# A two-layer graph network: half-length rows and three built columns in the second layer's gather loop

## The chip, the cores and the metric

The kernel runs on one core of a Trainium2 chip. The metric is the device time in microseconds of one execution. Engines are named as in the profile: PE (TensorE), ACT (ScalarE), DVE (VectorE), POOL (GpSimd), SP (SyncE, which here only issues DMAs).

## What is computed

Two graph layers over 12500 nodes of 32 features and 412500 edges sorted by destination. Before each, `h = relu(layernorm(x))`; each layer's output is added to `x`. The first is attention by a softmax over each node's incoming edges. The second, on which the change bears:

```python
x = h[src]; y = h[dst]; c = w_comp[etype]                  # 86 relations, 16 bases
xb = einsum('ei,bio->ebo', x, weight)
msg = einsum('eb,ebo->eo', c, xb)                          # = x @ W[etype]
x_hat = x @ A1_w.T + A1_b
y_hat = y @ A2_w.T + A2_b + rel_emb[etype]
a = tanh(relu(sum(x_hat * y_hat, -1) / sqrt(32)))
nei = segment_sum(a[:, None] * msg, dst)
curr = h[src[last_e]] @ self_loop_weight                   # last_e: last incoming edge of the node
h_new = relu(where(in_deg > 0, nei + curr, 0))
```

## The kernel before

**Layout.** The edges are cut into 128 runs of T = 3224, one per partition. Layer 0 takes them in 52 groups of 62 columns, layer 1 in 134 groups (`GROUPS1`) of 24 columns (`K1`) and a tail of 8 (`KT`). A column is one edge on each partition. Most columns come by an indirect DMA issued by POOL (`gather`, L683), which reads one row per partition from a table in DRAM. In layer 0 a row has 33 words. Some of layer 0's columns are not gathered but built: PE multiplies one-hot masks with the table that is held in SBUF in bf16 parts (L967), DVE picks the right one of 13 candidates.

**The table of layer 1.** Between the layers (about 3590 to 4003 us) the kernel computes, for each of the 98 nodes of a partition, `h1` and its product with all relations' matrices (PE L1017 and L1018), evicts it (ACT L858 to L864, DVE L1405) to a tile `tb` and stores it (SP L600). A table row serves 16 relations (`R8`; six rows a node): 16 words of bias products, 32 of `x_hat`, 32 of the self-loop product, 16 x 32 of messages, W1 = 592 words. A node's stored part has 3232 words. The `y_hat` of each node is stored too, and scattered to where its edges start.

**One group of layer 1.** POOL gathers `KG` = 23 columns into `g1`, which has two buffers: gathers for group g+2 wait until DVE has used group g (`s_g1_free`). The 24th column is built one group ahead. Who does what:
- ACT, in `edges1(g)`: `choose(g+1)` makes the one-hot masks (eight squares L895, one L896, two relus L898 and L899); the tanh (L913); a copy of the self part (L915); `relation` (L881); `fill(g+1)`: copies the picked row's transpose to `xT` (L903), waits for the products, copies the coefficients (L906) and the node part (L907); then, after DVE's scan, `y_starts(g+1)` (L884 to L888) and the copy to `r1` (L923).
- PE, in `base(g)`: two code transposes (L1039, L1040), wait for the masks, 24 matmuls over the table (L1049) into `found1`, transpose of the picked row (L1053), product with the bases (L1055), node product (L1056), coefficients (L1057).
- DVE, in `messages(g)`: fills the `y` values by a scan (L1458), masks of the relation, logits (L1468 to L1470), four `copy_predicated` (L1475) which halve the 16 messages to one by the bits of the relation number, with `pick_row(g+1)` (L1439 to L1444) after the first; weighting (L1482), the sum by a scan (L1485), `build_row(g+1)` (L1449 to L1453), and it waits for `r1` before the next group.
- SP loads `y` values, relations and indices and stores `r1` (L628 to L634).

Each engine runs its own list in order; semaphores tie them. At the end a fix of the run borders, 98 gathers of each node's last edge (sums and self part), three DVE operations per seventh of the nodes (L1517 to L1519), and the output.

Of the kernel before, what the change touches and what calls it, by code (L numbers as in the profile page):

```python
# [15 lines left out]
bf16 = mybir.dt.bfloat16  # L16
# [23 lines left out]
KG = K1 - 1  # L40
# [4 lines left out]
R8 = 16  # L45
# [25 lines left out]
assert 2 * (GROUPS - NB + 1) == J and PB == R8 and GROUPS1 % 2 == 0 and 0 < KT < K1  # L71
assert J == LOWS * (HIGHS - 1) + TALL and COLS0 % BATCH == 0 and 2 * BATCH <= PC - AHEAD0 + 1 and HIGHS <= R8
# [15 lines left out]
def build(nc, x, src, dst, etype, attn_w, weight, w_comp, self_w, a1_w, a1_b, a2_w, a2_b, rel_emb, out):  # L88
# [14 lines left out]
    yhat_d = dram("y_hat", (NP, D))  # L103
    z1_d = dram("y_hat_at_starts", (EP, D))
    r1_d = dram("layer1_scans", (EP, 2 * D))

    with ExitStack() as ctx:
# [10 lines left out]
        yhat = agg[:, :, :].rearrange("p j c -> p (j c)")[:, 0:J * D].rearrange("p (j c) -> p j c", c=D)  # L118
        shared = sb("weights_and_zeros", [P, WC + 3 * WC // 2 + K * D // 2])
# [3 lines left out]
        zeros = shared[:, WC + 3 * WC // 2:WC + 3 * WC // 2 + K * D // 2]  # L123
# [6 lines left out]
        a1b = sb("a1_and_bias", [D, D + 1])  # L130
        wattn = sb("attention_weights", [P, 2 * D])
# [19 lines left out]
        ylast = sb("last_y_hat", [P, D])  # L151
# [53 lines left out]
        junk = sdst_e[:, 0:T]  # L205
        blocks = view(0, [SB, EB])
# [38 lines left out]
        hT = take([TB, P], bf16)  # L245
        centered = zeros[:, 0:JQ * D].rearrange("p (j c) -> p j c", c=D)
# [4 lines left out]
        z1, r1, r1t, contx, r1t_tail, contx_tail = (  # L251
            shared[:, at:at + n].rearrange("p (a b) -> p a b", b=b) for at, n, b in (
                (0, K1 * D, D), (K1 * D, 2 * K1 * D, 2 * D), (3 * K1 * D, D * (K1 + 1), K1 + 1),
                (4 * K1 * D + D, D * (K1 + 1), K1 + 1), (5 * K1 * D + 2 * D, D * (KT + 1), KT + 1),
                (5 * K1 * D + KT * D + 3 * D, D * (KT + 1), KT + 1)))
        lg = take([K1])
        av = take([K1])
        spare = h[:, :, :].rearrange("p j c -> p (j c)")
        pr = spare[:, 0:K1 * (D + R8)].rearrange("p (k c) -> p k c", c=D + R8)
        ct1 = spare[:, K1 * (D + R8):K1 * (D + R8) + 2 * P]  # L260
        cn1 = spare[:, K1 * (D + R8) + 2 * P:K1 * (D + R8) + 3 * P]
# [47 lines left out]
        zp = ps[:, 0:2, :].rearrange("p b c -> p (b c)")[:, 0:D * (K1 + 1)].rearrange("p (c k) -> p c k", k=K1 + 1)  # L309
# [1232 lines left out]
```

## Time and profile before

| | us |
|---|---|
| median of 3 runs | 8054.69 (8054.45 to 8059.46) |
| profiled execution | 8059.34 |
| its span, first to last instruction | 8057.5 |
| PE, DVE, ACT, POOL busy | 4557.2, 6079.7, 1762.7, 5825.8 |

A busy share is a mean over stages that differ. The stages: up to about 580 us the indices are prepared; to about 3550 us layer 0; to 4003 us the table; to about 7905 us the loop of layer 1; then the end. The views used below are the page, busy times by stage or by short windows, groups of instructions, waits, and the timeline of one group.

### The profile page before, as it was taken

The page shows a single profiled execution, that of the slowest core. Times are in us where ns is not written, and L with a number is a line of the kernel's source. Part 1 is how long each engine was busy: PE and PEld are TensorE (multiplying, and loading weights), DVE is VectorE, ACT ScalarE, POOL GpSimd, SP SyncE. Part 2 cuts the span into 40 slices and gives each one's busy share as a digit, 9 for nine tenths or more (in the row PEclk, how much of TensorE's full clock was granted, in tenths as well). Part 3 has the DMA queues.
Part 4 walks back from the last instruction along what each step waited for, and adds up shares of the span by engine and source line. Part 5 has one row for each costly group of instructions (what it writes and reads, how often), then busy time and mean ns, then how long its engine had stood idle before and what let it go on. Part 6 is the DMA issues. An engine that isn't in the chain of part 4 may idle for free.

```text
span 8057.5 us, 68499 instructions
## 1 busy us (share of the span) xinstructions
PE 4557.2 (57%) x22931; PEld 2398.0 (30%) x22964; DVE 6079.7 (75%) x7991; ACT 1762.7 (22%) x3756; POOL 5825.8 (72%) x6148
## 2 busy tenths in 40 slices
PE   0009999999999999967633333333333333333330
PEld 0005555555555555533311111111111111111110
DVE  8437667767767767765578888888888888888883
ACT  0001001101101101126522323333232323323330
POOL 6777777777777777744367777777777777777776
PEclk9999999999999999988866666566666665656655
DMA  4412222222222222239988888888888888888882
GB/s 103 122 42 51 63 51 51 63 51 51 63 51 51 63 51 51 63 106 402 392 255 285 285 285 285 285 285 285 285 284 285 284 285 285 284 285 284 286 284 85
DMA packets 499205, 1492.16 MB, mean 185 GB/s; under 512 B 163302, under 2 KB 224019, under 8 KB 478244
## 3 DMA queue, kind: packets, MB, share of 16 engines
q0 software_dynamic: 349440, 1012.48, 44.2%
q1 hardware_dynamic: 149411, 475.30, 15.5%
q8 instruction: 181, 2.97, 0.2%
q14 instruction: 173, 1.42, 0.1%
HBM read 1078.52 MB, written 407.69 MB: 184 GB/s over the span
## 4 chain that ended last, share of the span: by engine, by line
DVE 38%; PE 29%; POOL 15%; DMA 9%; issue 7%; ACT 2%; DVEq 0%; POOLq 0%; SPq 0%; ACTq 0%
PE ps L967 27%; DVE arena L1475 16%; POOL arena L683 14%; DMA arena<-layer_rows,edge_row_index 5%; DMA layer_rows<-arena 3%; DVE arena L1470 2%; DVE arena L1282 2%; DVE h_nodes L1290 2%; DVE arena L1266 2%; DVE h_nodes L1469 1%; DVE ps L1258 1%; DVE ps L1458 1%; DVE weights_and_zeros L1485 1%; POOL dst_score_at_starts L719 1%; DVE arena L1293 1%
## 5 line engine op out<-in xcount | busy, mean ns | idle before, releaser
L683 POOL DMA_INDIRECT arena<-layer_rows,edge_row_index x5642 | 5342.6, 947 | 1783.1 <-issue 1731.3
L967 PE MATMUL ps<-arena 128*128 128x396 bf16 (+1 forms) x10752 | 2737.4, 336 | 0.0
L1475 DVE COPY_PREDICATED arena<-ps,arena 128x6144 f32<-128x6144 uint32 (+3 forms) x540 | 1828.2, 3386 | 41.7
L967 PE MATMUL ps<-h_nodes,arena 128*128 128x396 bf16 (+1 forms) x5376 | 1806.6, 336 | 0.0
L1049 PE MATMUL ps<-aggregate_nodes,weights_and_zeros 128*128 128x384 bf16 (+1 forms) x1072 | 480.0, 448 | 1632.7 <-ACT aggregate_nodes L899 1632.7
L967 PEld LDWEIGHTS ps<-arena 128*128 128x128 bf16 x10752 | 1045.5, 98 | 783.6 <-issue 18.9
L1290 DVE TENSOR_TENSOR h_nodes<-ps,h_nodes 128x429 f32<-128x429 f32 x672 | 604.7, 900 | 810.7 <-PE ps L967 810.7
L1049 PEld LDWEIGHTS ps<-aggregate_nodes,weights_and_zeros 128*128 128x128 bf16 x1072 | 136.0, 127 | 1797.5 <-ACT aggregate_nodes L899 1668.0
L967 PEld LDWEIGHTS ps<-h_nodes,arena 128*128 128x128 bf16 x5376 | 524.1, 97 | 404.9 <-issue 9.8
L1282 DVE TENSOR_SCALAR arena<-ps,low_id 128x512 bf16<-128x512 f16 x1344 | 588.0, 479 | 22.4 <-PE ps L956 0.4
L818 ACT ACTIVATE ps<-arena 128x62 f32<-128x62 f32 x52 | 11.7, 226 | 2202.9 <-DVE arena L1254 2202.9
L1049 PE MATMUL ps<-h_nodes,weights_and_zeros 128*128 128x384 bf16 (+1 forms) x1072 | 475.7, 444 | 0.0
L1049 PE MATMUL ps<-weights_and_zeros 128*128 128x384 bf16 (+1 forms) x1072 | 466.2, 435 | 0.0
L1053 PE MATMUL ps<-identity,aggregate_nodes 128*32 128x128 f32 x134 | 51.0, 381 | 732.5 <-DVE aggregate_nodes L1444 732.5
L1293 DVE TENSOR_REDUCE arena<-h_nodes 128x33 f32<-128x429 f32 x672 | 403.3, 600 | 23.1
L1458 DVE TENSOR_TENSOR_SCAN ps<-weights_and_zeros,ps 128x800 f32<-128x800 f32 x135 | 245.7, 1820 | 228.8 <-ACT weights_and_zeros L923 228.8
L956 PE MATMUL ps<-identity_h,code 128*128 128x128 f16 x672 | 65.9, 221 | 475.6 <-DVE code L1274 389.6
L824 ACT ACTIVATE arena<-arena 128x2046 f32<-128x2046 f32 x52 | 202.8, 3901 | 466.8 <-DVE arena L1266 466.8
L1055 PE MATMUL ps<-aggregate_nodes 32*128 32x512 f32 x268 | 276.1, 1121 | 47.7 <-ACT aggregate_nodes L903 47.7
L895 ACT ACTIVATE weights_and_zeros<-ps,minus_low_id 128x128 bf16<-128x128 f16 x1072 | 287.6, 372 | 0.5 <-PE ps L1040 0.5
L1405 DVE COPY arena<-ps 128x512 f32<-128x512 f32 (+1 forms) x294 | 157.5, 575 | 161.6 <-SPq L608 93.9
L884 ACT ACTIVATE weights_and_zeros<-same_dst_as_before 128x768 f32<-128x768 f32 x135 | 113.4, 840 | 749.9 <-DVE weights_and_zeros L1485 749.9
(273 smaller groups left out, 5751.7 us busy)
## 6 DMA issues: line engine op xcount, KB each, us to landing
layer_rows<-arena SPq DMA_DIRECT2D x98, 1616.0 KB, 8.0
layer_scans<-weights_and_zeros SPq DMA_DIRECT2D x134, 768.0 KB, 5.4
arena<-layer_rows,edge_row_index POOLq DMA_INDIRECT x5642, 4.1
layer_scans<-arena SPq DMA_DIRECT2D x52, 1054.0 KB, 4.2
y_hat_at_starts<-weights_and_zeros SPq DMA_DIRECT2D x52, 992.0 KB
weights_and_zeros<-y_hat_at_starts SPq DMA_DIRECT2D x134, 384.0 KB, 5.7
layer_rows<-weights_and_zeros SPq DMA_DIRECT2D x49, 320.0 KB
edge_row_index<-row_of_edge SPq DMA_DIRECT2D x134, 12.0 KB, 5.5
```

Source lines behind the costliest of these rows:

```text
L683: pool.indirect_dma_start(tile, None, table, bass.IndirectOffsetOnAxis(ap=index, axis=0)) \
L824: act.activation(r0[:, :, 0:D + 1], by_edge(r0t), ACT.Copy).then_inc(s_r0, 1)
L895: act.activation(onehot1[:, a, :], codes_n, ACT.Square, bias=neglow[:, a:a + 1])
L967: ins = nc.tensor.matmul(found[col % 2][:, 0:wide], onehot[n % 2][:, a, c * P:(c + 1) * P], tparts[i][:, a, 0:wide], start=a == 0 and i == ...
L1049: ins = nc.tensor.matmul(found1[:, 0:wide * D], onehot1[:, a, :], rows, start=a == 0 and i == 0, stop=a == LOWS - 1 and i == PARTS0 - 1)
L1055: nc.tensor.matmul(based, xT[0:D, :], wbas.rearrange("i (b o) -> i o b", o=D), start=True, stop=True)
L1266: v.tensor_tensor_scan(flat(r0t[:, 0:D, :]), flat(x0x[:, 0:D, :]), flat(b0t), 0.0, ALU.mult, ALU.add) \
L1282: ins = v.tensor_scalar(onehot[n % 2][:, a, :], codes, lowid[:, a:a + 1], None, ALU.is_equal)
L1290: v.tensor_tensor(picked[col % 2].rearrange("p c a -> p a c"), found[col % 2].rearrange("p (a c) -> p a c", c=FP), spread(high0[g % 2][:, ...
L1293: done(v.tensor_reduce(g0[g % NB][:, KP + i, 0:FP], picked[col % 2], AX.X, ALU.add))
L1458: v.tensor_tensor_scan(flat(y), flat(same), flat(y), 0.0, ALU.mult, ALU.add).then_inc(s_z1_used, 1)
L1475: done(v.copy_predicated(rows[:, :, M1:M1 + half], spread(bits[i][:, 0:k], [P, k, half]), rows[:, :, M1 + half:M1 + 2 * half]))
```

## The change

A table row now serves 8 relations (11 rows a node) and holds 8 words of bias products, `h1` itself (32 words) with a constant 1, and 8 x 32 of messages: W1 = 297 words, 1188 bytes. `x_hat . y_hat` is computed as (h1, 1) . (A1b' y_hat): the node's `y` is stored multiplied by the first attention matrix, 33 words. The self-loop product is no longer in the rows: `r1` carries `h1`, and the product with `self_loop_weight` is made at the end for each node's last edge. DVE's selects become three, over 8 messages. Of the 24 columns of a group three are built (`NE` = 3, `KG` = 21): ACT's masks are three times as wide, PE does 72 matmuls and three times transpose, product and coefficients, DVE three picks and three builds. The built columns' codes go by DRAM from the first stage to this loop. The tiles `relp` move from PSUM to SBUF. The three searches have PSUM banks 2, 4 and 5.

```diff
-KG = K1 - 1
+NE = 3
+KG = K1 - NE
 NB = 4
 QUADS = GROUPS // NB
 F0 = D + 1
 W0 = D + 2
-R8 = 16
+R8 = 8
+NS = 16
 RP = -(-RELS // R8)
 SLOTS = RP * R8
 X1 = R8
-M1 = X1 + 2 * D
+Y = D + 1
+M1 = X1 + Y
 W1 = M1 + R8 * D
 STORED = (RP - 1) * W1 + M1 + (RELS - (RP - 1) * R8) * D
-CN = 3 * D + SLOTS
+S1 = Y + 1
+CN = S1 + SLOTS
...
             def choose(g):
                 act.wait_ge(s_spelled, g + 1)
                 if g > 0:
-                    act.wait_ge(s_found1, g)
+                    act.wait_ge(s_found1, NE * g)
                 for a in range(LOWS):
                     act.activation(onehot1[:, a, :], codes_n, ACT.Square, bias=neglow[:, a:a + 1])
-                act.activation(which_r, codes_r[0:RELS, :], ACT.Square, bias=neglow[0:RELS, 0:1]).then_inc(s_hot, 1)
+                act.activation(flat_e(which_r), codes_r[0:RELS, :], ACT.Square, bias=neglow[0:RELS, 0:1]).then_inc(s_hot, 1)
                 act.wait_ge(s_hot, 2 * g + 1)
                 act.activation(onehot1, onehot1, ACT.Relu, scale=-1.0, bias=unit)
-                act.activation(which_r, which_r, ACT.Relu, scale=-1.0, bias=unit[0:RELS, :]).then_inc(s_hot, 1)
+                act.activation(flat_e(which_r), flat_e(which_r), ACT.Relu, scale=-1.0, bias=unit[0:RELS, :]).then_inc(s_hot, 1)
 
             def fill(g):
-                act.wait_ge(s_turned, g + 1)
-                act.activation(xT[0:D, :], xTp, ACT.Copy).then_inc(s_xT, 1)
-                act.wait_ge(s_based, g + 1)
-                act.wait_ge(s_g1_free, g + 1)
-                act.activation(coef, coefp, ACT.Copy)
-                act.activation(g1[:, g % 2, KG, X1:M1], noded, ACT.Copy).then_inc(s_fill, 1)
+                for e in range(NE):
+                    act.wait_ge(s_turned, NE * g + e + 1)
+                    if NE * g + e > 0:
+                        act.wait_ge(s_based, NE * g + e)
+                    act.activation(xT, xTp, ACT.Copy).then_inc(s_xT, 1)
+                act.wait_ge(s_based, NE * (g + 1))
+                if g > 0:
+                    act.wait_ge(s_built, g)
+                act.activation(coef, coefp, ACT.Copy).then_inc(s_fill, 1)
...
             def base(g):
                 if g > 0:
                     pe.wait_ge(s_fill, g)
-                nc.tensor.transpose(codes_n, code_n[:, g:g + 1].to_broadcast([P, P]), identh[:, :])
-                nc.tensor.transpose(codes_r, code_r[:, g:g + 1].to_broadcast([P, P]), identh[:, :]) \
-                    .then_inc(s_spelled, 1)
+                for e in range(NE):
+                    nc.tensor.transpose(codes_n[:, e * P:(e + 1) * P], code_n[:, g, e:e + 1].to_broadcast([P, P]),
+                                        identh[:, :])
+                for e in range(NE):
+                    ins = nc.tensor.transpose(codes_r[:, e * P:(e + 1) * P],
+                                              code_r[:, g, e:e + 1].to_broadcast([P, P]), identh[:, :])
+                ins.then_inc(s_spelled, 1)
                 pe.wait_ge(s_hot, 2 * g + 2)
                 if g > 0:
                     pe.wait_ge(s_built, g)
-                for a in range(LOWS):
-                    wide = HIGHS if a < TALL else HIGHS - 1
-                    for i in range(PARTS0):
-                        rows = table1[i][:, a:a + LOWS * (wide - 1) + 1:LOWS, :]
-                        ins = nc.tensor.matmul(found1[:, 0:wide * D], onehot1[:, a, :], rows,
-                                               start=a == 0 and i == 0, stop=a == LOWS - 1 and i == PARTS0 - 1)
-                ins.then_inc(s_found1, 1)
-                pe.wait_ge(s_xrow, g + 1)
-                nc.tensor.transpose(xTp, xrow, ident[:, :]).then_inc(s_turned, 1)
-                pe.wait_ge(s_xT, g + 1)
-                nc.tensor.matmul(based, xT[0:D, :], wbas.rearrange("i (b o) -> i o b", o=D), start=True, stop=True)
-                nc.tensor.matmul(noded, xT, wn[:, :], start=True, stop=True)
-                nc.tensor.matmul(coefp, which_r, wrel, start=True, stop=True).then_inc(s_based, 1)
+                for e in range(NE):
+                    for a in range(LOWS):
+                        wide = HIGHS if a < TALL else HIGHS - 1
+                        for i in range(PARTS0):
+                            rows = table1[i][:, a:a + LOWS * (wide - 1) + 1:LOWS, :]
+                            ins = nc.tensor.matmul(found1[e][:, 0:wide * D], onehot1[:, a, e * P:(e + 1) * P], rows,
+                                                   start=a == 0 and i == 0, stop=a == LOWS - 1 and i == PARTS0 - 1)
+                    ins.then_inc(s_found1, 1)
+                for e in range(NE):
+                    pe.wait_ge(s_xrow, NE * g + e + 1)
+                    if e > 0:
+                        pe.wait_ge(s_xT, NE * g + e)
+                    nc.tensor.transpose(xTp, g1[:, g % 2, KG + e, X1:X1 + D], ident[:, :]).then_inc(s_turned, 1)
+                    pe.wait_ge(s_xT, NE * g + e + 1)
+                    nc.tensor.matmul(based[e], xT, wbas.rearrange("i (b o) -> i o b", o=D), start=True, stop=True)
+                    nc.tensor.matmul(coefp[:, e, :], which_r[:, e, :], wrel, start=True, stop=True).then_inc(s_based, 1)
...
+            def masks(g):
+                done(v.tensor_tensor(high1[:, :, 0:HIGHS], slots[:, 0:HIGHS].unsqueeze(1).to_broadcast([P, NE, HIGHS]),
+                                     spread(high_n[:, g, :], [P, NE, HIGHS]), ALU.is_equal))
+
+            def pick_row(g, e):
+                v.wait_ge(s_found1, NE * g + e + 1)
+                done(v.tensor_tensor(picked1, found1[e].rearrange("p (a c) -> p a c", c=D),
+                                     spread(high1[:, e, 0:HIGHS], [P, HIGHS, D]), ALU.mult))
+                v.tensor_reduce(g1[:, g % 2, KG + e, X1:X1 + D], picked1.rearrange("p a c -> p c a"), AX.X, ALU.add) \
+                    .then_inc(s_xrow, 1)
+                v.wait_ge(s_xrow, NE * g + e + 1)
+
+            def build_rows(g):
                 v.wait_ge(s_fill, g + 1)
-                v.tensor_tensor(by_base, based.rearrange("p (o b) -> p o b", b=BASES),
-                                coef[:, 0:BASES].unsqueeze(1).to_broadcast([P, D, BASES]), ALU.mult)
-                done(v.tensor_tensor(by_rel, g1[:, g % 2, KG, X1:X1 + D], coef[:, BASES:BASES + D], ALU.mult))
-                v.tensor_reduce(g1[:, g % 2, KG, M1:M1 + D], by_base, AX.X, ALU.add)
-                v.tensor_reduce(g1[:, g % 2, KG, 0:1], by_rel, AX.X, ALU.add).then_inc(s_built, 1)
+                done(v.tensor_tensor(by_rel, g1[:, g % 2, KG:K1, X1:M1], coef[:, :, BASES:BASES + Y], ALU.mult))
+                v.tensor_reduce(g1[:, g % 2, KG:K1, 0], by_rel, AX.X, ALU.add)
+                for e in range(NE):
+                    done(v.tensor_tensor(by_base, based[e].rearrange("p (o b) -> p o b", b=BASES),
+                                         coef[:, e, 0:BASES].unsqueeze(1).to_broadcast([P, D, BASES]), ALU.mult))
+                    ins = v.tensor_reduce(g1[:, g % 2, KG + e, M1:M1 + D], by_base, AX.X, ALU.add)
+                    if e < NE - 1:
+                        done(ins)
+                ins.then_inc(s_built, 1)
                 v.wait_ge(s_built, g + 1)
...
                 v.tensor_tensor(which[:, 0:k, :], spread(relp[b][:, 0:k], [P, k, R8]),
-                                slots[:, :].unsqueeze(1).to_broadcast([P, k, R8]), ALU.is_equal)
-                for i in range(3):
+                                slots[:, 0:R8].unsqueeze(1).to_broadcast([P, k, R8]), ALU.is_equal)
+                for i in range(2):
                     v.tensor_scalar(bits[i][:, 0:k], rel[:, b, 0:k], R8 >> (i + 1), None, ALU.bitwise_and)
-                done(v.tensor_scalar(bits[3][:, 0:k], rel[:, b, 0:k], 1, None, ALU.bitwise_and))
+                done(v.tensor_scalar(bits[2][:, 0:k], rel[:, b, 0:k], 1, None, ALU.bitwise_and))
+                if g + 1 < GROUPS1:
+                    masks(g + 1)
                 v.wait_ge(s_g1[b], landed)
                 rows, part = g1[:, b, 0:k, :], pr[:, 0:k, :]
-                v.tensor_tensor(part[:, :, D:D + R8], rows[:, :, 0:X1], which[:, 0:k, :], ALU.mult)
-                done(v.tensor_tensor(part[:, :, 0:D], rows[:, :, X1:X1 + D], by_edge(y), ALU.mult))
+                v.tensor_tensor(part[:, :, Y:LW], rows[:, :, 0:X1], which[:, 0:k, :], ALU.mult)
+                done(v.tensor_tensor(part[:, :, 0:Y], rows[:, :, X1:M1], by_edge(y), ALU.mult))
                 v.tensor_reduce(lg[:, 0:k], part, AX.X, ALU.add).then_inc(s_lg, 1)
-                v.tensor_copy(y[:, :, 0], r1t[:, :, K1])
-                for i in range(4):
+                v.tensor_copy(y[:, 0:D, 0], r1t[:, :, K1])
+                for i in range(3):
                     half = (R8 >> (i + 1)) * D
                     v.nop(nofuse=True)
                     done(v.copy_predicated(rows[:, :, M1:M1 + half], spread(bits[i][:, 0:k], [P, k, half]),
                                            rows[:, :, M1 + half:M1 + 2 * half]))
-                    if i == 0 and g + 1 < GROUPS1:
-                        pick_row(g + 1)
+                    if i < NE and g + 1 < GROUPS1:
+                        pick_row(g + 1, i)
...
+            for q in range(J // JQ):
+                pe.wait_ge(s_sums[q], sums_landed(q))
+                if q > 0:
+                    pe.wait_ge(s_xlastT, q)
+                for j in range(JQ):
+                    ins = nc.tensor.transpose(xTsp[:, j * P:(j + 1) * P], sums1[:, q * JQ + j, D:2 * D], ident[:, :])
+                ins.then_inc(s_xlast, 1)
+                pe.wait_ge(s_xlastT, q + 1)
+                if q > 1:
+                    pe.wait_ge(s_out, q - 1)
+                for j in range(JQ):
+                    ins = nc.tensor.matmul(selfp[q % 2][:, j, :], xTs[:, q % 2, j * P:(j + 1) * P], wself, start=True,
+                                           stop=True)
+                ins.then_inc(s_curr, 1)
...
-                v.wait_ge(s_agg1[q], 16 * JQ)
+                v.wait_ge(s_sums[q], sums_landed(q))
                 total = sums1[:, at, 0:D]
-                done(v.tensor_tensor(total, total, sums1[:, at, D:2 * D], ALU.add))
+                v.wait_ge(s_curr, q + 1)
+                done(v.tensor_tensor(total, total, selfp[q % 2], ALU.add))
```

Beside this: `tb` gets its column of ones once; `a2_w` and its bias are multiplied with `a1_w` in the first stage; the weights take 7 small loads in place of 10; DVE waits there for the store of the codes; the code that shifts the relation by 4 shifts by 3, over three columns of each group in place of one; SP loads the codes before the table's first store.

## Rows read from the trace of the kernel before

**Rows 1.** The page: busy time of each engine, share of the span, instructions.
```profile
PE 4557.2 (57%) x22931; PEld 2398.0 (30%) x22964; DVE 6079.7 (75%) x7991; ACT 1762.7 (22%) x3756; POOL 5825.8 (72%) x6148
```
**Rows 2.** Stages: length, busy PE PEld DVE ACT POOL, PEclk, DMA share, GB/s.
```profile
400.00:3500.00 3100.00, 2817.83 (x16702) 1600.86 (x16703) 2107.51 (x3641) 306.35 (x198) 2339.46 (x2465) 0.99 0.24 54
...
5000.00:6000.00 1000.00, 362.36 (x1146) 163.12 (x1146) 883.13 (x873) 303.11 (x732) 756.25 (x800) 0.60 0.89 285
```
**Rows 3.** Groups, gathers: 400 to 3500 us, then 4650 to 7850 us; busy, mean ns, idle before.
```profile
L683 POOL DMA_INDIRECT arena<-layer_rows,edge_row_index x2356 | 2232.9, 948 | 718.0 <-issue 718.0
...
L683 POOL DMA_INDIRECT arena<-layer_rows,edge_row_index x2560 | 2420.3, 945 | 779.9 <-issue 777.7 <-DMA edge_row_index<-row_of_edge 2.1
```
**Rows 4.** Waits, 4650 to 7850 us: waiting line, releaser, total, times, longest.
```profile
DVE h_nodes L1468 <- DMA arena<-layer_rows,edge_row_index: 107.7, 70, 2.8
```
**Rows 5.** Groups by form, 4650 to 7850 us: count, busy, mean ns, idle before.
```profile
L1475 DVE COPY_PREDICATED arena<-ps,arena 128x6144 f32<-128x6144 uint32 x111 | 784.2, 7064 | 0.0
...
L1049 PE MATMUL ps<-h_nodes,weights_and_zeros 128*128 128x384 bf16 x666 | 272.1, 409 | 0.0
...
L1449 DVE TENSOR_TENSOR aggregate_nodes<-ps,aggregate_nodes 128x512 f32<-128x512 f32 x112 | 77.4, 691 | 3.8
```
**Rows 6.** Timeline, ACT's part of a group up to PE's start: start, duration, idle before.
```profile
5031.46 0.84 ACT L884 ACTIVATE weights_and_zeros<-same_dst_as_before 128x768 f32<-128x768 f32 x1 [5.51 <-DVE weights_and_zeros L1485]
...
5034.58 2.15 ACT L895 ACTIVATE weights_and_zeros<-ps,minus_low_id 128x128 bf16<-128x128 f16 x8
5036.58 0.38 ACT L896 ACTIVATE aggregate_nodes<-ps,minus_low_id 86x128 f32<-86x128 f16 x1
...
5038.48 0.53 PE L1049 MATMUL ps<-aggregate_nodes,weights_and_zeros 128*128 128x416 bf16 x1 [12.08 <-ACT aggregate_nodes L899]
```
**Rows 7.** Timeline of one search (24 matmuls), the pick and the chain after it.
```profile
5010.69 0.53 PE L1049 MATMUL ps<-aggregate_nodes,weights_and_zeros 128*128 128x416 bf16 x1 [12.10 <-ACT aggregate_nodes L899]
...
5015.95 0.44 PE L1049 MATMUL ps<-h_nodes,weights_and_zeros 128*128 128x384 bf16 x1
5016.22 0.33 PE L1049 MATMUL ps<-weights_and_zeros 128*128 128x384 bf16 x1
...
5017.20 0.33 PE L1049 MATMUL ps<-weights_and_zeros 128*128 128x384 bf16 x1
...
5020.03 0.59 DVE L1442 TENSOR_TENSOR aggregate_nodes<-ps,aggregate_nodes 128x416 f32<-128x416 f32 x1
...
5021.56 0.40 PE L1053 MATMUL ps<-identity,aggregate_nodes 128*32 128x128 f32 x1 [4.04 <-DVE aggregate_nodes L1444]
...
5022.32 2.07 PE L1055 MATMUL ps<-aggregate_nodes 32*128 32x512 f32 x2 [0.36 <-ACT aggregate_nodes L903]
...
5024.31 0.69 PE L1056 MATMUL ps<-node_weights,aggregate_nodes 33*128 33x64 f32 x2
...
5024.93 0.66 PE L1057 MATMUL ps<-aggregate_nodes 86*128 86x48 f32 x2
...
5025.63 0.21 ACT L906 ACTIVATE aggregate_nodes<-ps 128x48 f32<-128x48 f32 x1 [3.36 <-PE ps L1057]
```
**Rows 8.** Short windows, columns as in rows 2; the last in the table's stage.
```profile
5017.00:5018.00 1.00, 0.53 (x4) 0.10 (x1) 1.00 (x1) 0.00 (x0) 0.70 (x2) 1.00 0.98 322
5020.00:5021.00 1.00, 0.00 (x0) 0.00 (x0) 0.93 (x3) 0.00 (x0) 0.80 (x1) 0.50 0.76 256
...
3700.00:3728.00 28.00, 22.21 (x114) 10.46 (x114) 15.13 (x36) 16.66 (x48) 13.93 (x14) 0.88 0.99 400
```
**Rows 9.** Single lines: count, duration ns min/median/max, first and last start, forms.
```profile
L884 ACT ACTIVATE weights_and_zeros<-same_dst_as_before x135: 415/843/845, 4044.3 to 7905.0; 128x768 f32<-128x768 f32 x134, 128x256 f32<-128x256 f32 x1
...
L1053 PE MATMUL ps<-identity,aggregate_nodes x134: 283/396/398, 4057.4 to 7869.1; 128*32 128x128 f32 x134
...
L1055 PE MATMUL ps<-aggregate_nodes x268: 1032/1070/1219, 4058.1 to 7870.9; 32*128 32x512 f32 x134
```
**Rows 10.** Timeline of the end: two transposes of the border fix.
```profile
7917.97 0.61 PE L1066 MATMUL ps<-identity,carry_in 128*32 128x128 f32 x2 [44.87 <-DVE carry_in L1500]
```

More of the change, by code:

```diff
@@ L205, in build @@
         junk = sdst_e[:, 0:T]
+        coded = sdst_e[:, 2400:2400 + 3 * GROUPS1 * NE // 2 + 1].bitcast(fp16)[:, 0:3 * GROUPS1 * NE]
+        coded_n, coded_h = (coded[:, i * GROUPS1 * NE:(i + 1) * GROUPS1 * NE] for i in range(2))
+        coded_r = coded[:, 2 * GROUPS1 * NE:3 * GROUPS1 * NE].rearrange("p (g e) -> p g e", e=NE)
         blocks = view(0, [SB, EB])
@@ L245, in build @@
         hT = take([TB, P], bf16)
+        of_built = take([3 * GROUPS1 * NE // 2 + 1]).bitcast(fp16)
+        code_n, high_n, code_r = (of_built[:, i * GROUPS1 * NE:(i + 1) * GROUPS1 * NE].rearrange(
+            "p (g e) -> p g e", e=NE) for i in range(3))
+        table1 = [take([J, D // 2], bf16)]
         centered = zeros[:, 0:JQ * D].rearrange("p (j c) -> p j c", c=D)
@@ L394, in build @@
         s_wplaced = sem("s_wplaced")
-        s_agg0 = [sem(f"s_agg0_{i}") for i in range(-(-(J - TB - 1) // (2 * TB)) + 1)]
+        s_sums = [sem(f"s_sums{i}") for i in range(-(-(J - TB - 1) // (2 * TB)) + 1)]
         s_h1 = sem("s_h1")
@@ L436, in build @@
         s_self = sem("s_self")
-        s_agg1 = [sem(f"s_agg1_{i}") for i in range(J // JQ)]
         s_out = sem("s_out")
@@ L749, in _ @@
             for j in range(AHEAD):
-                gather(agg[:, j, :], r0_d, last[:, j:j + 1], s_agg0[part_of[j]])
+                gather(agg[:, j, :], r0_d, last[:, j:j + 1], s_sums[part_of[j]])
             pool.wait_ge(s_zero1_d, ZEROED)
@@ L754, in _ @@
                 for i in range(j + AHEAD, min(j + AHEAD + 1, J)):
-                    gather(agg[:, i, :], r0_d, last[:, i:i + 1], s_agg0[part_of[i]])
+                    gather(agg[:, i, :], r0_d, last[:, i:i + 1], s_sums[part_of[i]])
                 pool.wait_ge(s_ev_act, 6 * j + 12)
@@ L783, in _ @@
             for j in range(J):
-                gather(sums1[:, j, :], r1_d, last[:, j:j + 1], s_agg1[j // JQ])
+                gather(sums1[:, j, :], r1_d, last[:, j:j + 1], s_sums[j // JQ])
         @block.scalar
@@ L946, in _ @@
                                  start=True, stop=True)
+            nc.tensor.matmul(ps[0:D + 1, 6, 3 * RELS:3 * RELS + Y], a2b[:, :], a1b[:, :], start=True, stop=True)
             nc.tensor.matmul(ps[0:D + 1, 6, 2 * RELS:3 * RELS], a1b[:, :], rel_t[:, :], start=True, stop=True) \
@@ L1059, in _ @@
             pe.wait_ge(s_we, 48)
             pe.wait_ge(s_table1, 1)
+            pe.wait_ge(s_codes_in, 16)
+            nc.tensor.matmul(relp1, rel_t[:, :], a1b[:, :], start=True, stop=True).then_inc(s_relw, 1)
+            pe.wait_ge(s_wrel1, 1)
             for g in range(GROUPS1):
@@ L1481, in messages @@
                 v.wait_ge(s_self, g + 1)
[L1482 removed]
+                v.tensor_tensor(by_edge(y[:, 0:D, :]), rows[:, :, M1:M1 + D], spread(avp[:, 0:k], [P, k, D]), ALU.mult) \
                     .then_inc(s_g1_free, 1)
                 v.wait_ge(s_g1_free, g + 3)
[L1485 removed]
+                v.tensor_tensor_scan(flat(scanned), flat(same[:, 0:D, :]), flat(y[:, 0:D, :]), 0.0, ALU.mult, ALU.add).then_inc(s_scan1, 1)
                 v.wait_ge(s_scan1, g + 1)
                 if g + 1 < GROUPS1:
[L1488 removed]
+                    build_rows(g + 1)
                 v.wait_ge(s_r1, g + 1)
[L1491 to L1492 removed]
+            v.wait_ge(s_codes_in, 16)
+            masks(0)
+            for e in range(NE):
+                pick_row(0, e)
+            build_rows(0)
             for it in range(0, PAIRS1):
```

208 lines of the change are left out of this document (114 added, 94 removed).

## The prediction, made before the change was run

> **What bounds the kernel now.** I read the page first. GpSimd (POOL) is busy 72% of the span and VectorE (DVE) 75%; neither share decides alone, since both are means over unlike stages [rows 1]. The table of stages then separates two long stages: layer 0 (400 to 3500 us) and the layer-1 loop, of which 5000 to 6000 us is a sample. In both POOL is busy 75 to 76% [rows 2]. The groups of gathers tell what that is: each gather lasts 0.945 to 0.948 us and is followed by 0.30 us of issue (779.9 / 2560 and 718.0 / 2356), in layer 0 with rows of 132 bytes and in layer 1 with rows of 2368 bytes [rows 3]. So a gather costs POOL 1.25 us whatever its size, and 800 gathers fill the 1000 us of the sample. The layer-1 loop has 23 gathers per group of 24 columns: 23 x 1.25 = 28.75 us. The first and last transpose of a picked row (L1053) lie 3811.7 us apart, 133 intervals, 28.66 us each [rows 9]: POOL sets the pace. But narrowly: DVE waited for gathers only 107.7 us in 111 groups, 1 us each [rows 4], and is busy 0.883 x 28.7 = 25.3 us of each.
>
> **What the change aims at.** Three columns are built instead of gathered: 21 gathers, 21 x 1.25 = 26.25 us. That alone would be worth 133 x 2.4 = 320 us. The halved row frees DMA, which bounds nothing here. It remains to see whether the other engines can run a group in 26.25 us.
>
> **DVE.** The 6144-element select goes (7.06 us); two more picks at 1.53 us (from L1442's start at 5020.03 to TensorE's at 5021.56) and two more builds of 2 x 0.69 us come, 5.8 us [rows 5, 7]; narrower masks and reduce save an estimated 0.6 us, waits between dependent steps cost about that. 25.3 - 7.06 + 5.8 + 0.6 = 24 to 25 us of work. DVE fits in 26.25 us.
>
> **ScalarE (ACT) and TensorE (PE) do not.** Their part of a group is a ring in the code, written in order on both: ACT's `choose` (one-hot masks), PE's search of the table, PE and ACT in turns through transpose, `xT`, base product and coefficients, ACT's `coef` copy in `fill`, then `y_starts` and the copy to `r1`, and only then the next `choose`. PE begins its search when the masks are there and ends with what `fill` waits for. Nothing of the ring overlaps the rest of it; before, it was shorter than DVE's and POOL's work and waited for them. Its terms now:
> - `choose`: before 3.90 us, 5034.58 to PE's start at 5038.48 [rows 6]. Eight squares and one relation mask go from 128 to 384 elements, two relus likewise (1024 to 3072, 128 to 384). ACT's slope is (843 - 415) / 512 = 0.836 ns per element [rows 9]. Added: 10 x 256 + 2048 = 4608 elements, 3.85 us. New: 7.75 us.
> - search: 72 matmuls for 24. A burst starts at the lower clock level (1.2 GHz) and goes over to 2.4 GHz within itself; the granted clock is 1.00 at its end and back at 0.50 three microseconds later [rows 8]. Spacing is (5015.95 - 5010.69) / 16 = 0.329 us low and (5017.20 - 5016.22) / 6 = 0.163 us high [rows 7]. The 384-wide ones average 409 ns [rows 5] between 530 at the low and 330 at the high level [rows 7], so about 0.41 of 18 are slow, with the six 416-wide ones 13.4 matmuls or 4.4 us. Between bursts PE rests 11.2 us in the new ring, so each burst starts low again. 13.4 x 0.329 + 58.6 x 0.163 = 14.0 us (bounds: rise at once 11.7, never 23.7).
> - three passes of the chain: at the low clock, transpose to product 0.76 us (5021.56 to 5022.32), product 1.99 us (to 5024.31), coefficients 0.70 us (5024.93 to ACT at 5025.63), of which about 0.6 before PE can go on; the node product between (0.62 us) is gone. 3.35 us a pass. They now follow directly on the burst, at the high clock; the shortest transpose, 283 ns against a median of 396 [rows 9], is what I read as one at that clock. Of the others the trace has no full row; halving the streamed part (estimate: 2 x 512 columns, 1.99 to 1.1 us; coefficients to 0.45; transpose and ACT's copy 0.64) gives 2.2 us a pass. I take 6.7 us for three, because they come without a pause behind the burst, and in the table stage, where PE has gaps too, the granted clock was 0.88 on average over 28 us [rows 8]. The other bound is 3 x 3.35 = 10.1 us.
> - `coef` copy 0.3, `y_starts` and `r1` 3.12 us (5031.46 to 5034.58) [rows 6] plus 0.05 for the 33rd column.
>
> Sum: 7.75 + 14.0 + 6.7 + 0.3 + 3.17 = 31.9 us. DVE is in time inside it: its last pick ends 1.5 us after the search, the weighting and scan 3.1 us later, before the 6.7 us of passes end. DVE's rows are built after `fill` (4.9 us), under ACT's next steps. POOL, with 26.25 us, starts to wait for buffers.
>
> So 133 x (31.9 - 28.66) = +431 us. **Around the loop:** the first row's preparation lengthens by 3.85 + 7.8 + about 1.5 us less 2.5 us for two gathers, +11 us. The last full group and the tail group of 8 lose their widest selects and the copy wait: -14 us. In the table stage DMA is busy 99% at 400 GB/s [rows 8], and a node's stored row goes from 3232 to 3203 words: 0.9% of 410 us, -4 us; ACT's and DVE's copies there are behind it. `y` rows of 33 for 32 words, three times the codes in the first stage, the codes' trip to DRAM and the fewer weight loads lie beside POOL's gathers there: I put them at 0, at most 5 us if the cover is gone. At the end, the last seventh needs 14 transposes at 0.21 us spacing (0.61 for two, 0.40 for one [rows 7, 10]), an ACT copy of 1792 elements (1.7 us) and 14 products of 0.3 to 0.6 us behind its last gather, less one addition: +13 us; the six earlier ones hide in the 17.5 us that the next seventh's 14 gathers take.
> The profiled execution took 8059.3 us (span 8057.5); 8059.3 + 431 + 11 - 14 - 4 + 13 = 8496. The median of the runs is 4.6 us lower: about **8490 us**.
>
> **Two rules against these rows.** ACT's masks take a bias by pointer. Eight squares of 128 take 2.00 us here (5034.58 to 5036.58 [rows 6]), 0.25 each, so 0.46 each at 384. The Trainium skill, ScalarE: Activation LUTs, What ACT_TABLE_LOAD costs, gives about 280 ns + 0.833 ns per element with some 93 ns of overlap; as an estimate from that page a square of 384 costs 0.51 us, and the total comes out some 50 us higher. The row decides.
> For the search the rows give 0.163 us per matmul at the high clock. The Trainium skill, TensorE: Matmul & The Clock Gate, Back-to-back issue gap, has 131 ns for 512 columns in a sustained stream; by it the search would shrink by some 2.5 us a group, and the time by 330 us. The rows of this trace stand against it.
>
> **Rivals.**
> - Faster: the ring is hidden and POOL stays the bound. It decides the case if the ring takes under 28.66 us, and at 26.25 or less it gives 8055 - 320 + 6 = about 7740 us. It needs the next masks or the passes to overlap the search, which the order of the code excludes, or an ACT and PE much quicker than their rows. For it: POOL's exact pace now. Chance 0.05.
> - Low clock in the passes: PE has gaps there while ACT copies and waits. Then 10.1 for 6.7, ring 35.3 us: +885 us, 8945. For it: before the change no product ran under 1032 ns [rows 9], and the clock had fallen 3 us after the burst of 5017 [rows 8]. Against: PE had idled over 4 us ahead of them [rows 7]. Chance 0.25, with mixtures between.
> - Clock high nearly at once in every burst: search 11.7 us, ring 29.6, +125 us: 8185. Against it stands every burst of the loop. Chance 0.05.
> - That DVE is the bound (24 to 25 us) or that the change leaves the time alone: 0.02; the ring would have to end within 0.15 us of today's 28.66.
> - The forecast, ring 30.7 to 33.2 us: 0.63, its own range 8330 to 8665.
>
> **How the numbers follow.** The likeliest case gives 8490. The range takes in the forecast and nearly all of the low-clock case: 8330 to 8930 us. The three runs of before lie within 0.06%, so over 0.2% (16 us) counts as a change: slower 0.94, same 0.01, faster 0.05.
>
> **What would show it.** Right: POOL's gathers stop for several us in each group and it waits for DVE (a buffer); ACT and PE are released by each other, L1049's group trebles, its mean near 380 ns; the group period is near 32 us; DMA's share of time falls to about half; DVE waits for PE before its second and third pick. The passes' product shows about 0.6 us per half if the clock is high, 1.07 if low. Wrong: gathers without gaps at 1.25 us (then the ring is hidden), or `choose` under 7 us, or passes that begin before the third search ends. A period over 34 us would say low clock in the passes.

## The result, and the profile after

| | median us | ratio to before, 95% interval |
|---|---|---|
| before | 8055.1 | |
| changed | 8795.4 (8793.7 to 8797.4) | 1.092 [1.090, 1.094] |

The change costs 740 us. The forecast, 8490, had the sign and the mechanism; the size fell above the forecast case's own 8330 to 8665, between it and the 8945 of the rival of the low clock in the passes. It lies in the stated range (to 8930) only because that range took in most of this rival. The profiled execution took 8797.4 us with a span of 8795.6 us.

The page of the changed kernel: busy times, the chain that ended last, two groups of section 5 (count | busy us, mean ns | idle before).
```profile
PE 6273.5 (71%) x31269; PEld 3253.4 (37%) x31302; DVE 5879.6 (67%) x8795; ACT 2326.3 (26%) x3899; POOL 5571.9 (63%) x5880
...
PE 60%; ACT 18%; DVE 10%; POOL 5%; DMA 4%; issue 3%; POOLq 0%; SPq 0%; DVEq 0%; ACTq 0%
...
L708 POOL DMA_INDIRECT arena<-layer_rows,edge_row_index x5374 | 5089.1, 947 | 2764.5 <-issue 2688.5
```
Against [rows 1] POOL and DVE are less busy in a longer span; PE gained 1716 us of work and ACT 564. The chain now runs 78% over PE and ACT. A gather still takes 947 ns, but the idle time before it grew: POOL waits.

The same sample of the loop as in [rows 2], and the waits of 5000 to 8000 us (88 groups: waiting line, releaser, total, times, longest).
```profile
5000.00:6000.00 1000.00, 659.44 (x2701) 309.23 (x2699) 703.13 (x918) 381.73 (x653) 583.33 (x618) 0.70 0.45 131
```
```profile
ACT aggregate_nodes L936 <- PE ps L1102: 1631.1, 264, 13.1
POOL arena L708 <- issue: 1244.8, 1807, 8.6
...
PE ps L1095 <- ACT aggregate_nodes L929: 875.6, 88, 10.0
DVE aggregate_nodes L1528 <- ACT aggregate_nodes L940: 428.0, 87, 5.3
...
DVE aggregate_nodes L1520 <- PE ps L1095: 396.4, 262, 3.1
```
In every group ACT waits 18.5 us for PE's transposes (1631.1 / 88; up to 13.1 of them for the search) and PE 10.0 us for ACT's masks (L929): two engines that take turns. DVE waits for both, 9.4 us a group; before it waited 1 us for gathers [rows 4] and 1.7 us for `r1` (188.8 us in 111 groups). No engine is full. DMA's share fell from 0.89 to 0.45 and bought nothing.

One group of the changed kernel in order of time: end of the search, the three passes (L1102 transpose, L1104 product, L1105 coefficients), ACT's coefficients (L940), starts and `r1`, the masks, the next search.
```profile
5501.67 0.33 PE L1095 MATMUL ps<-weights_and_zeros 128*128 128x384 bf16 x1
...
5501.84 0.27 PE L1102 MATMUL ps<-identity,arena 128*32 128x128 f32 x1
...
5502.46 1.96 PE L1104 MATMUL ps<-aggregate_nodes 32*128 32x512 f32 x2 [0.36 <-ACT aggregate_nodes L936]
...
5504.36 0.42 PE L1105 MATMUL ps<-aggregate_nodes 86*128 86x49 f32 x2
...
5504.61 0.28 PE L1102 MATMUL ps<-identity,arena 128*32 128x128 f32 x1
...
5505.25 2.07 PE L1104 MATMUL ps<-aggregate_nodes 32*128 32x512 f32 x2 [0.36 <-ACT aggregate_nodes L936]
...
5507.71 0.41 PE L1102 MATMUL ps<-identity,arena 128*32 128x128 f32 x1
...
5508.48 2.07 PE L1104 MATMUL ps<-aggregate_nodes 32*128 32x512 f32 x2 [0.36 <-ACT aggregate_nodes L936]
...
5511.18 0.29 ACT L940 ACTIVATE aggregate_nodes<-ps 128x147 f32<-128x147 f32 x1 [2.75 <-PE ps L1105]
...
5514.54 3.86 ACT L925 ACTIVATE weights_and_zeros<-ps,minus_low_id 128x384 bf16<-128x384 f16 x8
...
5522.29 0.53 PE L1095 MATMUL ps<-arena,weights_and_zeros 128*128 128x416 bf16 x1 [9.95 <-ACT aggregate_nodes L929]
```
The masks take 5522.29 - 5514.54 = 7.75 us, as worked out before. Coefficients, starts and `r1` take 3.36. The passes take 2.77, 3.10 and 3.47 us, 9.34 to the coefficients, where 6.7 was expected. Over the groups between 5000 and 7000 us the means are: period 34.13, coefficients to search 11.12, search 13.67, passes 2.78 + 3.10 + 3.47 us, and nothing is left over. The whole loop agrees: L940, the last ACT step of a ring, stands 4537.5 us from first to last.
```profile
L940 ACT ACTIVATE aggregate_nodes<-ps x134: 292/292/293, 4079.8 to 8617.3; 128x147 f32<-128x147 f32 x134
```
4537.5 / 133 = 34.12 us, against 28.66 [rows 9].

The clock in the passes (columns as in [rows 2], the granted clock third from the end):
```profile
5503.00:5504.00 1.00, 1.00 (x2) 0.00 (x0) 0.93 (x3) 0.00 (x0) 0.00 (x0) 1.00 0.00 0
...
5506.00:5507.00 1.00, 1.00 (x2) 0.00 (x0) 0.66 (x1) 0.00 (x0) 0.70 (x2) 0.50 0.00 0
```
The first product runs at 1.00 and the second, from 5505.25, at 0.50, and they take 1.96 and 2.07 us. So two things differ from the forecast: the clock falls during the second pass, and a product at the high clock is hardly shorter than one at the low. The experiments say which counts.

### The profile page after: what moved, and what is told of

It reads as the page before. It is cut to its first block, busy times and chain, and to the rows that moved or that the text cites. A ratio compares the mean times of both kernels' runs of the same rounds, so it can differ in the third digit from the quotient of the medians.

```text
span 8795.6 us, 86677 instructions
## 1 busy us (share of the span) xinstructions
PE 6273.5 (71%) x31269; PEld 3253.4 (37%) x31302; DVE 5879.6 (67%) x8795; ACT 2326.3 (26%) x3899; POOL 5571.9 (63%) x5880
## 4 chain that ended last, share of the span: by engine, by line
PE 60%; ACT 18%; DVE 10%; POOL 5%; DMA 4%; issue 3%; POOLq 0%; SPq 0%; DVEq 0%; ACTq 0%
PE ps L1008 25%; PE ps L1095 21%; PE ps L1104 9%; ACT weights_and_zeros L925 6%; ACT weights_and_zeros L928 4%; POOL arena L708 4%; DMA layer_rows<-arena 3%; ACT weights_and_zeros L956 2%; PE ps L1105 2%; DVE arena L1351 1%; DVE h_nodes L1359 1%; DVE arena L1335 1%; DVE ps L1327 1%; ACT weights_and_zeros L911 1%; ACT aggregate_nodes L936 1%
## 5 line engine op out<-in xcount | busy, mean ns | idle before, releaser
L708 POOL DMA_INDIRECT arena<-layer_rows,edge_row_index x5374 | 5089.1, 947 | 2764.5 <-issue 2688.5
L1095 PE MATMUL ps<-arena,weights_and_zeros 128*128 128x384 bf16 (+1 forms) x3216 | 1167.2, 363 | 1329.0 <-ACT aggregate_nodes L929 1329.0
L1095 PE MATMUL ps<-weights_and_zeros 128*128 128x384 bf16 (+1 forms) x3216 | 1142.1, 355 | 0.0
L1095 PE MATMUL ps<-h_nodes,weights_and_zeros 128*128 128x384 bf16 (+1 forms) x3216 | 1139.5, 354 | 0.0
L1095 PEld LDWEIGHTS ps<-arena,weights_and_zeros 128*128 128x128 bf16 x3216 | 334.9, 104 | 1621.5 <-ACT aggregate_nodes L929 1364.4
L1560 DVE COPY_PREDICATED arena<-ps,arena 128x3072 f32<-128x3072 uint32 (+2 forms) x405 | 904.5, 2233 | 28.5 <-DVE arena L1522 0.9
L1104 PE MATMUL ps<-aggregate_nodes 32*128 32x512 f32 x804 | 817.8, 1106 | 143.9 <-ACT aggregate_nodes L936 143.9
L844 ACT ACTIVATE ps<-arena 128x62 f32<-128x62 f32 x52 | 11.7, 225 | 2203.4 <-DVE arena L1323 2203.4
L925 ACT ACTIVATE weights_and_zeros<-ps,minus_low_id 128x384 bf16<-128x384 f16 x1072 | 516.8, 590 | 1.8 <-PE ps L1084 1.8
L1095 PEld LDWEIGHTS ps<-weights_and_zeros 128*128 128x128 bf16 x3216 | 332.4, 103 | 293.6 <-issue 75.4
L1095 PEld LDWEIGHTS ps<-h_nodes,weights_and_zeros 128*128 128x128 bf16 x3216 | 333.0, 104 | 263.5 <-issue 75.2
```

Of the source, the lines that this page charges most:

```text
L708: pool.indirect_dma_start(tile, None, table, bass.IndirectOffsetOnAxis(ap=index, axis=0)) \
L925: act.activation(onehot1[:, a, :], codes_n, ACT.Square, bias=neglow[:, a:a + 1])
L1095: ins = nc.tensor.matmul(found1[e][:, 0:wide * D], onehot1[:, a, e * P:(e + 1) * P], rows, start=a == 0 and i == 0, stop=a == LOWS - 1 and ...
L1104: nc.tensor.matmul(based[e], xT, wbas.rearrange("i (b o) -> i o b", o=D), start=True, stop=True)
L1560: done(v.copy_predicated(rows[:, :, M1:M1 + half], spread(bits[i][:, 0:k], [P, k, half]), rows[:, :, M1 + half:M1 + 2 * half]))
```

## The experiments

**How many columns to build.** The first two set the change's own constant, `NE`.
```diff
-NE = 3
+NE = 1
```


> The change with NE = 1: half-length rows, h1 in them, self loop at the end, but one built column as before (23 gathers a group). Theory (POOL's 1.25 us per gather whatever its size, and the ring of ACT and PE hidden): 23 x 1.25 = 28.75 us a group, the whole within 20 us of before, 8040 to 8070 us; the ring is about 3.4 + 3.9 + 6 + 3.5 = 17 us. DVE's work falls to about 18.5 us a group, and that brings nothing. Rival (gathers wait for DMA, so shorter rows speed them up): under 1.25 us a gather and under 7900 us. Rival (the new rows cost by themselves, in DVE or in the new end): over 8150 us.

Measured 8058.2 us, ratio 0.9993 [0.998, 1.000]. All of the new layout without a further built column neither gains nor loses: 133 intervals from 4059.3 to 7863.1, 28.6 us each.
```profile
L940 ACT ACTIVATE aggregate_nodes<-ps x134: 211/211/212, 4059.3 to 7863.1; 128x49 f32<-128x49 f32 x134
```
Halved rows and 7 us less DVE work a group don't move a loop that waits for POOL's 23 gathers.

```diff
-NE = 3
+NE = 2
```


> The change with NE = 2: 22 gathers, two built columns. Theory: the ring is 3.4 (coefficients, starts, r1) + 5.8 (masks: 3.90 + 2304 elements x 0.836 ns) + 9.6 (48 matmuls, 10 of them at 0.329 and 38 at 0.165 us) + 6.2 (two passes) = 25.0 us, under POOL's 22 x 1.25 = 27.5 us. POOL sets the pace: 8055 + 133 x (27.5 - 28.66) = 7900 us. Rival (each built column costs what the third appears to cost, in DVE's builds): halfway between before and after, about 8400 us.

Measured 7919.3 us, ratio 0.982 [0.981, 0.984]: 1.8% less than before. Its gathers from 5500 to 6500 us (count | busy, mean ns | idle before):
```profile
L708 POOL DMA_INDIRECT arena<-layer_rows,edge_row_index x797 | 754.3, 946 | 246.6 <-issue 246.6
```
797 gathers in 1000 us are 1.255 us each, without gaps; the period is 27.54 us. The 19 us over the expected time are not accounted for one by one; the kernel before ran at 8064 us beside it, 9 us over its usual. DVE waits for gathers 691.9 us in 119 of the groups from 4200 to 7500 us, so the ring is in time. So two built columns leave POOL the bound, and the third makes the ring the bound: a built column isn't dear in itself.

**Why the product is slow at the high clock.**
```diff
-nc.tensor.matmul(based[e], xT, wbas.rearrange("i (b o) -> i o b", o=D), start=True, stop=True)
+nc.tensor.matmul(based[e], xT, wbas, start=True, stop=True)
...
-based[e].rearrange("p (o b) -> p o b", b=BASES)
+based[e].rearrange("p (b o) -> p o b", o=D)
```


> Only the order in which the product reads the base matrices: contiguous in SBUF (b, o) in place of strides of 32 words (o, b); DVE reads the result with the stride instead. It tells why the product of 2 x 512 float32 columns takes 1.89 us with the granted clock at 1.00 and 1.99 us at 0.50. If the strided read is what holds it, a product at 1.00 falls to about 1.1 us, a pass to 2.0 us, the ring by at least 0.8 us: about 8690 us or less. If float32 matmuls of this length take the same at both clock levels for another reason, the pass stays 2.8 and 3.1 us and the time 8795 within 20 us (DVE's strided reads may move it by a few us up).

Measured 8624.0 us, ratio 1.069 [1.068, 1.071]: 171 us less than the changed kernel. Its three passes:
```profile
5511.54 0.27 PE L1102 MATMUL ps<-identity,arena 128*32 128x128 f32 x1
5512.17 1.12 PE L1104 MATMUL ps<-aggregate_nodes 32*128 32x512 f32 x2 [0.36 <-ACT aggregate_nodes L936]
...
5513.48 0.28 PE L1102 MATMUL ps<-identity,arena 128*32 128x128 f32 x1
...
5515.42 0.27 PE L1102 MATMUL ps<-identity,arena 128*32 128x128 f32 x1
5516.05 2.07 PE L1104 MATMUL ps<-aggregate_nodes 32*128 32x512 f32 x2 [0.36 <-ACT aggregate_nodes L936]
```
The pair now takes 1.12 us at the high level and the same 2.07 us at the low one; a pass at the high level takes 1.94 us. So it was the read with a stride of 32 words that kept the product at 1.96 us at the high clock; at the low one the order of the read makes no difference. DVE's product with the coefficients, which reads PSUM with the stride now, stays at 689 ns. The passes come to 1.94 + 2.24 + 3.42 = 7.60 us, 1.75 less. The group gains only 1.29 us (32.84), since the search lengthened from 13.67 to 14.13: its clock now rises 2.7 to 5.9 us after its start, 4.2 on average, where in the changed kernel it rose after 3.0 to 3.2 us every time.

**PE kept from resting.**
```diff
                 ins.then_inc(s_spelled, 1)
+                for i in range(44 if g > 0 else 0):
+                    nc.tensor.matmul(ps[:, 7, 64:64 + 12 * D], identb[:, :], table1[0][:, 2:2 + 8 * 11 + 1:8, :],
+                                     start=True, stop=True)
                 pe.wait_ge(s_hot, 2 * g + 2)
```


> 44 more matmuls of 384 columns a group between the code transposes and the wait for the masks, into a bank that nothing reads, so that PE doesn't rest while ACT makes the masks; th and avp lie in SBUF for that. Theory (ring of ACT and PE, with the search's first 3.3 us at the low clock): the search falls from 13.67 to 11.8 us, the passes a little, the group from 34.1 to about 32 us, the whole to 8795 - 133 x 2 = about 8530 us although PE does 60% more matmuls. Rival (PE isn't in the path that sets the pace): 8795 us or more.

Measured 8584.3 us, ratio 1.064 [1.063, 1.066]: 211 us less, with 44 useless matmuls a group, and 54 us over the expected 8530.
```profile
5510.20 9.08 PE L1089 MATMUL ps<-arena,identity_b 128*128 128x384 bf16 x44
...
5520.38 0.36 PE L1099 MATMUL ps<-arena,weights_and_zeros 128*128 128x416 bf16 x1 [1.10 <-ACT aggregate_nodes L930]
5532.35 0.33 PE L1099 MATMUL ps<-weights_and_zeros 128*128 128x384 bf16 x1
5532.52 0.27 PE L1106 MATMUL ps<-identity,arena 128*32 128x128 f32 x1
```
The search starts at the high level and lasts 12.13 us. The passes stay at 2.80 + 2.99 + 3.45 us: 21 us of dense matmuls ahead of them, with one pause of 1.1 us, don't keep the clock up through them. The low start of the search costs 13.67 - 12.13 = 1.54 us a group, less than the 2.3 us reckoned before (14.0 against 11.7 at best): the 11.7 were too low.

**Does the order alone make the ring the bound?** ACT's masks for the next group go between its copies in the passes; the codes are spelled behind the search; each third of the search waits for its own bank only; `th` and `avp` go to SBUF and the codes to a bank of their own. All work stays. The parts of this edit weren't tried one by one.
```diff
             def fill(g):
                 for e in range(NE):
...
                     act.activation(xT, xTp, ACT.Copy).then_inc(s_xT, 1)
+                    if g + 1 < GROUPS1:
+                        if e < 2:
+                            squares(g + 1, range(4 * e, 4 * e + 4))
+                        else:
+                            hots(g + 1)
...
                 act.activation(coef, coefp, ACT.Copy).then_inc(s_fill, 1)
+                if g + 1 < GROUPS1:
+                    which_rel(g + 1)
...
             def edges1(g, b, turn, k=K1, scanned=r1t, k_next=K1, same=contx, y=zp):
-                if g + 1 < GROUPS1:
-                    choose(g + 1)
```


> Same work as the changed kernel, other order: ACT makes the next group's masks between its copies in the three passes of this group (four squares, four squares, the wide relu), PE spells the next codes right after the search, and each third of the search waits only for its own bank's build; th, avp in SBUF, codes in their own bank. Theory (time is set by the ring because nothing of it overlaps): about 6.6 of the 7.75 us of masks leave the ring. Search 13.7 + passes 9.4 + coefficients and the relation's mask 1.6 = about 25 us; through DVE's builds, selects and picks and the third pass also about 25 us; POOL's 21 x 1.25 = 26.25 us becomes the bound: about 8060 - 133 x 2.4 + 20 = 7760 us, 1000 us under the changed kernel. Rival (DVE's added builds and picks set the pace of the changed kernel): it stays near 8790 us. Rival (a built column costs more than a gather whatever the order): above 8060 us.

Measured 7772.9 us, ratio 0.965 [0.963, 0.966]: 1023 us under the changed kernel, 286 under the one before. The timeline shows squares (L926) and the wide relu (L932) between the `xT` copies (L945), and the coefficients (L954) right behind:
```profile
5520.83 0.27 ACT L945 ACTIVATE aggregate_nodes<-ps 32x128 f32<-32x128 f32 x1 [5.26 <-PE ps L1122]
5521.01 1.94 ACT L926 ACTIVATE weights_and_zeros<-ps,minus_low_id 128x384 bf16<-128x384 f16 x4
5523.62 0.27 ACT L945 ACTIVATE aggregate_nodes<-ps 32x128 f32<-32x128 f32 x1 [0.67 <-PE ps L1122]
5523.79 1.94 ACT L926 ACTIVATE weights_and_zeros<-ps,minus_low_id 128x384 bf16<-128x384 f16 x4
5526.86 0.27 ACT L945 ACTIVATE aggregate_nodes<-ps 32x128 f32<-32x128 f32 x1 [1.12 <-PE ps L1122]
5527.03 2.84 ACT L932 ACTIVATE weights_and_zeros<-weights_and_zeros,chunk_scalars 128x3072 bf16<-128x3072 bf16 x1
5529.88 0.29 ACT L954 ACTIVATE aggregate_nodes<-ps 128x147 f32<-128x147 f32 x1
```
From coefficients to search it takes 2.41 us in place of 11.12, and the period is 26.45 us, POOL's 21 gathers and 0.2 us. POOL gathers without gaps (0.3 us of issue before each, as in [rows 3]); the 0.2 us are in the gathers, whose mean from 4200 to 7500 us is 956 ns here for 945 in the changed kernel. The DVE rival falls with this: DVE does the same work in 26.45 us, though it is busy 90% of the time. Nor is the ring of ACT and PE much shorter than POOL's work: DVE never waits for a gather here.

> e5_masks_in_passes together with the contiguous reading of e3_plain_order. Theory: with POOL as the bound at 26.25 us a group the shorter product brings nothing more: within 20 us of e5_masks_in_passes. If the ring is still the bound there, the time falls by 0.5 to 1.3 us a group, 70 to 170 us.

Its edit is those of e3 and e5 together. Measured 7782.6 us, ratio 0.966 [0.964, 0.967], 10 us over e5. The shorter product brings nothing once POOL is the bound: its gathers have no gaps, DVE now waits for gathers (81.0 us, 49 times from 4200 to 7500 us, in e5 never), PE waits for DVE's picks (129.7 us for 0.6), and so the passes stay as long as in e5. The 10 us go with the gathers, whose mean is 962 ns for 956; why some of them last longer is open. Single periods there last up to 29.6 us.

**Which engine's work costs time.** Two additions of nearly the same length to the changed kernel.
```diff
+                for _ in range(3):
                     done(v.tensor_tensor(part[:, :, 0:Y], rows[:, :, X1:M1], by_edge(y), ALU.mult))
```


> The changed kernel with DVE's product of h1 and y (792 elements, 0.97 us) made three times: 1.94 us more DVE work a group ahead of the logits. Theory (ring of ACT and PE): DVE waits for PE before its second and third pick anyway, so nothing: 8795 us within 20. Rival (DVE sets the pace, or shares it): + 133 x 1.94 = + 258 us, 9053 us.

Measured 8794.2 us, ratio 1.091 [1.090, 1.093]: nothing, though DVE is the busiest engine of the loop, at 70% (PE: 66%). The work went into DVE's waits for the search, 131.7 us in the changed kernel and 71.4 us here (5500 to 6500 us, first the changed kernel, then this run):
```profile
DVE aggregate_nodes L1528 <- ACT aggregate_nodes L940: 143.2, 29, 5.3
DVE aggregate_nodes L1520 <- PE ps L1095: 131.7, 88, 2.8
```
```profile
DVE aggregate_nodes L1528 <- ACT aggregate_nodes L940: 147.6, 30, 5.3
DVE aggregate_nodes L1520 <- PE ps L1095: 71.4, 87, 1.7
```

```diff
                 for a in range(LOWS):
                     act.activation(onehot1[:, a, :], codes_n, ACT.Square, bias=neglow[:, a:a + 1])
+                if g > 1:
+                    act.wait_ge(s_hot, 2 * g)
+                for a in range(4 if g > 0 else 0):
+                    act.activation(extra[a], codes_n, ACT.Square, bias=neglow[:, a:a + 1])
```


> The changed kernel with four more squares of 384 elements in the masks, written to a tile that nothing reads: 4 x 0.47 = 1.9 us more ACT work a group, as much as e7_more_dve adds to DVE. ACT is busy 37% in the loop, the least of the four. Theory (it lies in the ring): + 133 x 1.9 = + 250 us, 9045 us. Rival (the busiest engine sets the pace, so ACT's work is free): 8795 us within 20.

Measured 9120.6 us, ratio 1.132 [1.130, 1.134]: +325 us on the engine that is busy 38%. Coefficients to search grew by 1.87 us as expected (11.12 to 12.99). The search grew by 0.66 us (13.67 to 14.33), since its clock rises after 4.6 us on average in place of 3.2, and the second pass shortened by 0.08: 133 x (1.87 + 0.66 - 0.08) = 326 us. So the added work costs 249 us and the clock's timing most of the rest. The wait in the edit is for ACT's own last step of the group before.

## Why the prediction was right, and where its size was off

- **POOL's 1.25 us a gather whatever the row's size**: held; 28.6, 27.5 and 26.45 us for 23, 22 and 21 gathers in e1, e2 and e5.
- **The ring of ACT and PE takes the place of POOL's work as the bound**: shown, by e5 (same work, other order and finer waits, -1023 us) and by the pair e7 and e8.
- **Masks, 7.75 us**: measured 7.75. Coefficients, starts and `r1`, 3.47: measured 3.36. ACT's slope per element [rows 9] carried over to tiles three times as wide. The squares are spaced (5514.54 to the next line's start at 5518.24) / 8 = 0.46 us, as the row gave and not the 0.51 us that the prediction estimated from the Trainium skill, ScalarE: Activation LUTs, What ACT_TABLE_LOAD costs.
- **Search, 14.0 us**: measured 13.67. The rise came at 3.2 us after the start, not 4.4. In e3 and e8 the same 72 matmuls took 14.13 and 14.33 us with the rise at 4.2 and 4.6, so this steady early rise is luck worth 0.5 to 0.7 us a group. At the high level the spacing was the 0.163 us of [rows 7], so the other figure weighed there, 131 ns for 512 columns from the Trainium skill, TensorE: Matmul & The Clock Gate, Back-to-back issue gap, doesn't hold here either. (What it would have been worth was also off: 58.6 x 32 ns is 1.9 us a group, not 2.5.)
- **Passes, 6.7 us: the step that failed.** Measured 9.35, which is 133 x 2.65 = 352 us: more than the 305 us between forecast and result, the search having taken 44 us less. "Halving the streamed part" at the high clock was wrong: the product takes 1.96 us there for 2.07, because of its strided read (e3: 1.12 with a plain one). This was the larger share. With all three passes as the first one (2.77 us) the term would still be 8.3 us and more. The rest is the clock, which fell in the second pass; the rival of the low clock had that right, and its 10.1 us were nearly reached by a sum of both causes. The prediction's sign for this rival, a period over 34 us, came true (34.12) though the clock was the smaller part. The price of the product at the high clock stood in the trace of before, where the prediction found "no full row": the first group of the loop has transpose and product at the granted clock of 1.00.
```profile
4057.42 0.29 PE L1053 MATMUL ps<-identity,aggregate_nodes 128*32 128x128 f32 x1 [1.64 <-DVE aggregate_nodes L1444]
4058.07 1.96 PE L1055 MATMUL ps<-aggregate_nodes 32*128 32x512 f32 x2 [0.36 <-ACT aggregate_nodes L903]
...
4059.00:4060.00 1.00, 1.00 (x3) 0.04 (x1) 0.00 (x0) 0.00 (x0) 0.69 (x2) 1.00 0.86 204
```
In the window's row the granted clock is third from the end. No product under 1032 ns [rows 9] said the same. I read that as "always low", although the shortest transpose (283 ns) showed the clock to be high at times.
- **DVE in time inside the ring**: held, e7; its wait for the coefficients was up to 5.3 us a group.
- **Around the loop**: the first coefficients come 18.9 us later (4060.9 to 4079.8), of which 7 were expected. The table's last store begins 3.8 us later than before (4006.76 for 4002.98 us at SP), not 4 earlier: the stored bytes fell by 0.9% and the stage's time didn't. The first search took 14.9 us. From the last coefficients to the end: 178.3 us for 184.4, 6 less, with 1 less expected. The sum: 133 x 5.45 + 18.9 - 6.1 = 738 us, the whole difference of the spans.

## What to carry to other kernels

When work moves from the engine that sets the pace to others, add up the longest ring of waits that it joins, not the engines' busy time: here no engine was over 71% busy and the ring cost 740 us. Try the order of a ring before its work: here the same work, with the next group's masks placed in the gaps of this group's passes, ran 1023 us faster, while the shorter product gained 171. And raise such a constant one step at a time: 2 built columns gained 1.8% where 3 lost 9.2%.

## What the runs showed of the hardware that I had not expected

- A float32 matmul of 512 columns whose moving operand is read with a stride of 32 words (128 bytes) takes 1.96 us a pair with the granted clock at 1.00 and 2.07 at 0.50; read contiguously, 1.12 and 2.07.
- The clock fell to 0.50 during a chain of transpose, copy, float32 product and small product that followed directly on 13.7 us (changed kernel) and 21 us (e4) of dense matmuls, and useless matmuls ahead of a burst paid for themselves (-211 us).
- In the changed kernel the clock's rise came 3.0 to 3.2 us after the start of every search between 5000 and 7000 us, in e3, e5 and e8 at any point between 2.6 and 6.0 us. Why it is so even there wasn't tried. It means that an edit can move the time of this loop by up to 0.7 us a group, some 90 us, through the clock's timing alone, and differences between e3, e8 and the changed kernel hold such a part.
